# Two cross attentions whose row maxima are joined to the queries and whose scores are formed a second time, transposed

## The reference

```python
# layer 1                                            # layer 3: the same with biases on q, k, v, no mask, and
q = heads(x @ Wq); k = heads(ctx @ Wk); v = heads(ctx @ Wv)
scores = einsum('bhid,bhjd->bhij', q, k) * hd ** -0.5
scores = where(mask[:, None, None, :], scores, max_neg)
out = einsum('bhij,bhjd->bhid', softmax(scores), v).reshape(B, N, 256)
return out @ Wo                                      # relu(out @ W1 + b1) @ W2 + b2
```

## Time and profile before

| | us |
|---|---|
| runs | 1791.15, 1791.43, 1797.4 (median 1791.43) |
| profiled execution, span | 1785.6 |
| layer 1's cross attention, first scores to the last batch's `output_rows` | 659.05 to 831.19 |
| layer 3's, the same | 1351.67 to 1535.98 |
| busy over the span | PE 1579.5, DVE 941.3, ACT 717.5, POOL 409.0 |

### The profile page before, as it was taken

One profiled execution on the slowest core, in us unless ns is written; L12 is line 12 of the kernel. 1 busy time (PEld: TensorE's weight loads), 2 busy tenths in 40 slices (PEclk: granted clock), 3 DMA queues, 4 the chain that ended last, 5 costly groups with the idle time before them and its releaser, 6 DMA issues.

```text
span 1785.6 us, 40853 instructions
## 1 busy us (share of the span) xinstructions
PE 1579.5 (88%) x14786; PEld 1305.9 (73%) x14786; DVE 941.3 (53%) x2546; ACT 717.5 (40%) x1675; POOL 409.0 (23%) x627
## 2 busy tenths in 40 slices
PE   7998998799987879998797788997988999899998
PEld 6876776678975657776687566775876777689897
DVE  3665877511116657777110562556345667565864
ACT  3334876232323336652222314551755556211110
POOL 2224776500004421112000233432121111000101
PEclk9998999999998999998899798998998999999999
DMA  5343000278951011102686001001001000033232
GB/s 212 147 151 121 28 27 19 106 279 300 321 185 35 1 53 44 29 15 87 254 290 228 13 1 58 28 27 48 1 1 66 23 26 15 24 96 117 81 108 68
DMA packets 41852, 166.72 MB, mean 93 GB/s; under 512 B 5985, under 2 KB 16865, under 8 KB 30177
## 3 DMA queue, kind: packets, MB, share of 16 engines
q1 hardware_dynamic: 39392, 159.14, 25.7%
q0 software_dynamic: 2304, 5.51, 1.0%
HBM read 140.21 MB, written 24.41 MB: 92 GB/s over the span
## 4 chain that ended last, share of the span: by engine, by line
PE 70%; DVE 12%; issue 7%; DMA 3%; POOL 3%; ACT 3%; SPq 1%; DVEq 0%; POOLq 0%; ACTq 0%
PE bank L1688 7%; PE bank L1701 6%; PE bank L1268 6%; PE bank L1630 4%; PE bank L1255 4%; PE bank L1631 4%; PE bank L1632 4%; PE bank L1282 3%; PE bank L795 2%; PE bank L804 2%; PE bank L1238 2%; PE bank L1243 2%; PE bank L896 1%; PE bank L782 1%; DMA xrow<-slots 1%
## 5 line engine op out<-in xcount | busy, mean ns | idle before, releaser
L2053 ACT ACTIVATE arena<-big,nm 112x375 f32<-112x375 f32 x384 | 215.9, 605 | 29.5 <-DVE nm L2894 16.4
L1268 PEld LDWEIGHTS bank<-cst,arena 112*125 112x125 f32 x1152 | 146.6, 192 | 54.0 <-issue 29.0
L1268 PE MATMUL bank<-cst,arena 112*125 112x112 f32 x1152 | 168.0, 283 | 8.8 <-ACT big L2063 5.0
L3150 POOL TENSOR_TENSOR mv<-mv,cst 112x1 f32<-112x1 f32 x88 | 20.1, 228 | 607.3 <-DVE mv L2283 607.3
L2202 ACT ACTIVATE htile<-bank,wup 128x128 f32<-128x128 f32 x280 | 79.7, 368 | 189.7 <-PE bank L1688 189.6
L1688 PE MATMUL bank<-xtile,wup 128*128 128x128 f32 x1120 | 132.8, 278 | 0.3 <-DVE xtile L2997 0.2
L1688 PEld LDWEIGHTS bank<-xtile,wup 128*128 128x128 f32 x1120 | 129.8, 194 | 1.0 <-DVE xtile L2997 0.9
L3013 DVE COPY yrow<-bank 128x256 f32<-128x256 f32 x35 | 14.8, 424 | 217.5 <-PE bank L1701 217.5
L1701 PE MATMUL bank<-wdn,htile 128*128 128x256 f32 x560 | 126.3, 379 | 0.0
L2897 DVE TENSOR_SCALAR_CACHE_REDUCE big<-bank 112x375 f32<-112x375 f32 x192 | 96.0, 543 | 35.3 <-PE bank L1255 33.6
L1701 PEld LDWEIGHTS bank<-wdn,htile 128*128 128x128 f32 x560 | 103.9, 190 | 12.8
(11 more groups left out here) (359 smaller groups left out, 3571.7 us busy)
## 6 DMA issues: line engine op xcount, KB each, us to landing
wup<-in_moe_up SPq DMA_DIRECT2D x35, 1028.0 KB, 7.3
wdn<-in_moe_dn SPq DMA_DIRECT2D x35, 1024.0 KB, 6.1
vspace<-in_ring SPq DMA_DIRECT2D x40, 512.0 KB, 4.2
ctxs<-parts SPq DMA_DIRECT2D x30, 564.0 KB, 3.9
slots<-mlpw SPq DMA_DIRECT2D x11, 1024.0 KB, 6.5
parts<-ctxs SPq DMA_DIRECT2D x8, 564.0 KB, 3.1
xrow<-slots SPq DMA_DIRECT2D x35, 128.0 KB, 5.0
slots<-yrow SPq DMA_DIRECT2D x35, 128.0 KB, 7.0
```

Source lines behind the costliest of these rows:

```text
L1268: mm = pe.transpose(bank[4 + (3 * g + t) % 2][0:KT, j * T:(j + 1) * T], c_pr[:, g, j, t * KT:(t + 1) * KT], ident[0:T, 0:T])
L2053: nc.scalar.activation(c_pr[:, g, j, :], c_sc[:, g % 2, j, :], ACT.Exp, bias=nm[:, p, h:h + 1], scale=-1.0).then_inc(cexp_done, 1)
```

## The change

In layers 1 and 3 the program `cross_joined` takes the place of `cross` on every engine. VectorE only reads each bank of scores and stores the row minimum into `j_nm` (nothing is kept of the scores themselves). At the start of the next batch's steps TensorE transposes the minima of all 16 heads (`maxima`), and VectorE makes `j_q` from them and the negated queries (`maxima_in`): each head's 32 rows now hold 16 query rows and one row with the maxima. The keys are stored twice (`j_k`, one copy for even and one for odd heads), with ones in the row that meets the maxima, so that a second product (`scores_t`: for each of three thirds of the context 16 matmuls of 32 contraction rows, 125 x 112) gives scores minus maximum, already transposed. ScalarE takes the exponential from PSUM (12 of 125 x 448 per batch; in layer 1 the mask is a bias per context row, read from a new small input `mask_columns`). `transposes` and `tile` are gone. `values` runs once per batch, 48 matmuls, in the fourth step of the following batch. In that step the order on TensorE is: scores, queries of b + 1, values of b - 1, first half of the keys of b + 1, two thirds of the value rows of b, `rows_t` of b - 2. Banks: row scores in 3, 0, 1, 2, transposed scores in 3, 4, 5, 6 (6 is `OT`; 4 and 5 also take keys and value rows). Both parts now drain in 8 steps. `cross` is left for layer 0 alone, otherwise as it was. The core of the diff, with unchanged branches and small helpers cut:

```diff
+        self.ctx, self.joined = True, not clip and not qk_norm
...
+self.per.update({"c16": 16, "n1": 1, "m1": 1 if mlp else 0})
+        cols += [("keyhalf", 2), ("keyadd", 4)] if self.joined else [("bk", 2)]
...
+ROW_BANKS, TURNED_BANKS = (3, 0, 1, 2), (3, 4, 5, 6)
...
+    def scores(b, g, p):
+        if g == 0:
+            pe.wait_ge(cqm_ready, at(sub, "c1", b, 1))
+        if g % 2 == 0:
+            pe.wait_ge(ck_done, at(sub, "c2", b, g // 2 + 1))
+        pe.wait_ge(nexp_done, at(sub, "p12", b - 1, 4 * g - 3))
+        for j in range(4):
+            pe.wait_ge(cmax_ready, at(sub, "c16", b, 4 * g + j - 3))
+            if ROW_BANKS[j] == 0 and routed:
+                pe.wait_ge(route_in, 6 + routed)
+            rows = slice(32 * j, 32 * j + 32)
+            pe.matmul(bank[ROW_BANKS[j]][0:T, 0:S2], c_qm[rows, p, g // 2, g % 2, :], j_k[rows, p, g // 2, g % 2, :],
+                      start=True, stop=True).then_inc(cs_ready, 1)
+    def maxima(b, more):
+        pe.wait_ge(anm_clear, 3 + sub.index // 10)
+        pe.wait_ge(cmax_ready, at(sub, "c16", b, 16))
+        if more:
+            pe.wait_ge(cq_done, at(sub, "c1", b + 1, 1))
+        pe.wait_ge(xt_done, xt_at(sub, b - 2))
+        for g in range(4):
+            mm = pe.transpose(TL[:, g * T:(g + 1) * T], j_nm[:, g, :], ident[0:T, 0:T])
+        mm.then_inc(anm_ready, 1)
+    def scores_t(b, t, p, more):
+        pe.wait_ge(anm_done, at(sub, "n1", b, 1))
+        if more:
+            pe.wait_ge(cmax_ready, at(sub, "c16", b + 1, 4 * t + 1))
+        if t == 0:
+            pe.wait_ge(cv_done, at(sub, "c3", b, 3))
+            pe.wait_ge(cot_in, at(sub, "t1", b, 0))
+        for g in range(4):
+            for i in range(4):
+                if g == 0:
+                    pe.wait_ge(nexp_done, at(sub, "p12", b, 4 * t + i - 3))
+                rows = slice(32 * i, 32 * i + 32)
+                mm = pe.matmul(bank[TURNED_BANKS[i]][0:KT, g * T:(g + 1) * T],
+                               j_k[rows, p, g // 2, g % 2, t * KT:(t + 1) * KT], j_q[rows, g, :], start=True, stop=True)
+                if g == 3:
+                    mm.then_inc(ns_ready, 1)
+    def values(b, p):
+        pe.wait_ge(v_zero, 2)
+        pe.wait_ge(nexp_done, at(sub, "p12", b, 12))
+        for g in range(4):
+            for t in range(3):
+                for j in range(4):
+                    h = head_of(g, j)
+                    mm = pe.matmul(OT[32 * j:32 * j + 32, g * T:(g + 1) * T], vbuf[:, p, t, 32 * h:32 * h + 32],
+                                   j_p[:, t, j, g * T:(g + 1) * T], start=(t == 0), stop=(t == 2))
+        mm.then_inc(nv_done, 1)
...
+    def idle(b, n):
+        if isinstance(b, int) and b >= B:
+            pe.wait_ge(cmax_ready, at(sub, "c16", B - 1, 16))
+            for _ in range(n):
+                warm(bank[1], 256)
...
+    def step(b, g, p, back, more, one, two):
+        if g == 0:
+            if one:
+                maxima(b - 1, back[0])
+            if back[0]:
+                scores(b, g, p)
+                if one:
+                    pe.wait_ge(anm_done, at(sub, "n1", b - 1, 1))
+                value_rows(b, p, 0, TL)
+            if one:
+                idle(b, 2)
+                scores_t(b - 1, 0, 1 - p, back[0])
+            if two:
+                if back[0]:
+                    pe.wait_ge(cv_done, at(sub, "c3", b, 1))
+                elif one:
+                    pe.wait_ge(anm_done, at(sub, "n1", b - 1, 1))
+                else:
+                    pe.wait_ge(xt_done, xt_at(sub, b - 3))
+                output_rows(sub, b - 2)
+        if g == 1:
+            if back[0]:
+                scores(b, g, p)
+                if two:
+                    pe.wait_ge(con_step, at(sub, "t2", b - 1, 0))
+                else:
+                    pe.wait_ge(cv_done, at(sub, "c3", b, 1))
+                keys(b, p, 1, TL)
+            if one:
+                idle(b, 4)
+                scores_t(b - 1, 1, 1 - p, back[0])
+            if two:
+                if back[0]:
+                    pe.wait_ge(ck_done, at(sub, "c2", b, 2))
+                idle(b, 0 if one else 2)
+                output_columns(sub, b - 2)
+        if g == 2:
+            if back[0]:
+                scores(b, g, p)
+            if two:
+                if sub.mlp:
+                    hidden(b - 2)
+                else:
+                    project_rows(sub, b - 2)
+            if one:
+                idle(b, 2)
+                scores_t(b - 1, 2, 1 - p, back[0])
+            if two and sub.mlp:
+                project_hidden(b - 2)
+        if g == 3:
+            if back[0]:
+                scores(b, g, p)
+            if more:
+                if two:
+                    pe.wait_ge(ln_dve, u + 3 * (b - 2) + 1)
+                else:
+                    pe.wait_ge(ck_done, at(sub, "c2", b, 2))
+                q_in(b + 1, 1 - p, TL)
+            if one:
+                idle(b, 4)
+                values(b - 1, 1 - p)
+            if more:
+                keys(b + 1, 1 - p, 0, bank[4])
+            if back[0]:
+                pe.wait_ge(cq_done, at(sub, "c1", b, 1))
+                for t in (1, 2):
+                    value_rows(b, p, t, bank[5][:, (t - 1) * DM:t * DM])
+            if two:
+                if more:
+                    pe.wait_ge(cq_done, at(sub, "c1", b + 1, 1))
+                idle(b, 0 if one else 4)
+                rows_t(sub, b - 2, p)
+        if sub.index == 4 and isinstance(b, int) and b >= B - 2:
+            route(b, g)
+    cross_steps(pe, step, 8)
...
+    def keys(b, p, m, src):
+        act.wait_ge(ck_ready, at(sub, "c2", b, m + 1))
+        for e in range(2):
+            ins = nc.scalar.activation(j_k[:, p, m, e, :], src[:, 0:S2], ACT.Identity, scale=w(sub, "keyhalf")[:, e:e + 1],
+                                       bias=w(sub, "keyadd")[:, 2 * m + e:2 * m + e + 1])
+        ins.then_inc(ck_done, 1)
...
+    def exps(b, t, p):
+        if t == 0:
+            act.wait_ge(nv_done, at(sub, "v1", b, 0))
+            if sub.mask:
+                act.wait_ge(crow_ready, b + 1)
+        for i in range(4):
+            act.wait_ge(ns_ready, at(sub, "p12", b, 4 * t + i + 1))
+            src = bank[TURNED_BANKS[i]][0:KT, 0:4 * T]
+            if sub.mask:
+                ins = nc.scalar.activation(j_p[:, t, i, :], src, ACT.Exp, bias=mask_add[:, p, t:t + 1])
+            else:
+                ins = nc.scalar.activation(j_p[:, t, i, :], src, ACT.Exp)
+            ins.then_inc(nexp_done, 1)
...
     def step(b, g, p, back, more, one, two):
+        if g == 0 and back[0]:
+            value_rows(b, p, 0, 1, TL)
+        if g == 1 and back[0]:
+            keys(b, p, 1, TL)
+        if g == 2 and two and sub.mlp:
             hidden(b - 2)
+        if g < 3 and one:
+            exps(b - 1, g, 1 - p)
+        if g == 3:
+            if more:
+                q_in(b + 1, 1 - p, TL)
+                keys(b + 1, 1 - p, 0, bank[4])
+            if back[0]:
+                value_rows(b, p, 1, 2, bank[5])
+            if two:
+                rows_in(B + sub.base["row"], b - 2)
         if sub.index == 4 and isinstance(b, int) and (b, g) in ((B - 2, 3), (B, 0)):
             route_exps(1, 0 if b < B else 1)
+    cross_steps(act, step, 8)
...
+    def scores_in(b, g, p, js):
+        for j in js:
+            h = 4 * g + j
+            dve.wait_ge(cs_ready, at(sub, "c16", b, h + 1))
+            apart(dve)
+            at_max = j_nm[:, g, 32 * j + 16 - 16 * (g % 2):32 * j + 17 - 16 * (g % 2)]
+            src = bank[ROW_BANKS[j]][0:T, 0:S2]
+            if sub.mask:
+                if h == 0:
+                    dve.wait_ge(crow_ready, b + 1)
+                    apart(dve)
+                dve.wait_ge(cmax_ready, at(sub, "c16", b, h - 1))
+                apart(dve)
+                ins = dve.tensor_tensor_reduce(j_sum[:, j % 2, :], src, j_row[:, p, :], 1.0, -LOWEST,
+                                               ALU.add, ALU.min, at_max)
+            else:
+                ins = dve.tensor_reduce(at_max, src, AX_X, ALU.min)
+            ins.then_inc(cmax_ready, 1)
+    def maxima_in(b, p):
+        dve.wait_ge(anm_ready, at(sub, "n1", b, 1))
+        dve.scalar_tensor_tensor(out=j_q.rearrange("p g n -> p (g n)"), in0=c_qm[:, p, :, :, :].rearrange("p m e n -> p (m e n)"),
+                                 scalar=-1.0, in1=TL[:, 0:4 * T], op0=ALU.mult, op1=ALU.add).then_inc(anm_done, 1)
...
+    def step(b, g, p, back, more, one, two):
+        if g == 0:
+            if two:
+                output_in(sub, b - 2, nv_done, at(sub, "v1", b - 1, 0))
+            if one:
+                maxima_in(b - 1, 1 - p)
+            if sub.index == 4 and isinstance(b, int) and b == B:
+                route(sub, 7.5)
+            if back[0]:
+                scores_in(b, g, p, range(4))
+        if g == 1:
+            if back[0]:
+                scores_in(b, g, p, (0,))
+            if two:
```

(40 more changed lines are left out.)

395 lines of the change are left out of this document (211 added, 184 removed).

## The result

The changed kernel takes 1819.43 us (median of 4 runs, 1817.3 to 1819.71) against 1794.41 (4 runs, 1791.15 to 1798.04) on the same chip: ratio 1.0136, 95% interval 1.0116 to 1.0155. The forecast was 1790 with a range of 1772 to 1808; the time lies above the range. The profiled span grew from 1785.6 to

A forecast was written before the change was run, and what follows sets the result against it. The order and length of TensorE's pieces were taken to bound both stages. Layer 1's +3.2 and layer 3's -4.4 us sum to -1.2, from 1785.6 to 1784.4 profiled, forecast as a median of 1790, range 1772 to 1808.

The forecast's parts named there:

- Bound and throughput: Both stages: TensorE's pieces set the time; its work falls 2.95 us per batch, giving 35 us over 12 batches if gapless.
- A steady batch, the waits: Layer 1's steady batch: TensorE waits about 4.5 us in sum, including 1.5 at the keys and 1.25 at `maxima`.
- Rival (b): Steady batches: half of the waits at keys and `maxima` vanish, 17 us less, 1773 in all; chance 0.28.
- A steady batch, the prices: TensorE's time from piece to piece: four row scores 0.83 us, keys 0.8, transposed scores 1.05; VectorE reads after 1.07.
- the walk: One steady layer 1 batch followed piece by piece from `maxima`: period 20.5 us against 20.15 before.
- Rival (c): Handovers between engines around bank 3 cost more than taken; 0.5 us more each gives 1811; chance 0.19.
- the ring of bank 3: Three times per batch: TensorE's product goes to ScalarE, back to TensorE's scores, then to VectorE; last scores wait 0.8 us.
- Fill: Batches 0 and 1 of both stages: batch 0 takes 11.9 us, batch 1 17.4; -3.3 in layer 1, -3.4 in layer 3.
- Rival (d): Steady periods: TensorE's waits lower its granted clock to a mean of 0.96, +14 us, 1804 in all; chance 0.08.
- Batches 6 and 7, drain: Layer 1's end: batches 6 and 7 take 46.0 us with routing's 6 us as before, -0.3; the drain +3.4.
- Start: Before the first scores: one key product less, -1.0 us per stage.
- Tail, layer 3's end: Layer 1's routing tail +3 us, bounds 0 and 4; layer 3's batch 7 with drain 39.1 against 35.6, +3.5.

The follow-up runs named there:

- e5: Changed kernel with VectorE normalising the output of two batches ago before the first new row minimum; ratio 1.0054 to the kernel before, layer 1 period 20.87 us.
- e6: Changed kernel with `rows_t` and its copy ahead of the keys in the fourth step; ratio 1.0064 to the kernel before, layer 1 period 21.16 us.
- e3: Changed kernel with TensorE's instructions of both joined stages written out instead of looped; ratio 1.0122 to the kernel before, layer 1 period 21.30 us.
- e12: Changed kernel with early second keys and warm products in batch 0, normalisation before row minima, `rows_t` before keys, TensorE written out; ratio 0.9907 to the kernel before.
- e4: Changed kernel with layer 1's row minima taken by a plain reduction without the mask's row; ratio 1.0119 to the kernel before, layer 1 period 21.75 us.
- e8: Changed kernel with layer 1's routing operations one step later in batch 7 and behind batch 6's normalisation in the drain; ratio 1.0107 to the kernel before.

## Why the prediction was wrong

**Bound and throughput.** Right: in all steady batches TensorE's own order sets the time, VectorE and ScalarE are under 12 us of 22. The waits eat what the removed transposes give.

**A steady batch, the waits.** Right in place, close in size: e5 took 1.31 and e6 1.02 out of the period, where the forecast had 1.5 and 1.25. All waits of the period shown add up to 3.5 us (0.57, 1.23, 0.24, 0.70, 0.79), against the forecast's about 4.5, so they can't be what made the period longer. Rival (b) said that half of the two large waits would not be there; the changed kernel has them in full.

**A steady batch, the prices.** This is the step that failed most: "From one piece's start to the next on TensorE: four row scores 0.83". The prices came from rows in which TensorE had not waited. In the loop of the changed kernel three of the four row scores take 1.12 to the next piece, and the transposed scores of the first step 1.38. e3 and e12 show that this goes when the loop is written out, 1.2 us of TensorE's work per batch (18.51 to 17.28). A second part was in the walk from piece to piece itself. The throughput count leaves 20.05 - 2.95 = 17.1 us of work, and e3's 17.28 bears it out; the walk, 20.5 with 4.5 of waits, has only 16.0, and the two were not compared. One price in it was misread, the keys at 0.8; a timeline of before has 0.95 from the keys to the next piece:

```profile
718.77 1.11 PE L1238 MATMUL bank<-ctxs,kv 128*128 128x376 f32 x5
719.72 1.02 PE L1268 MATMUL bank<-cst,arena 112*125 112x112 f32 x8
```

In the changed kernel they take 1.06 and 0.97, twice per batch. VectorE's first read lies 1.45 behind the first scores, not 1.07; e4 takes 0.22 of these 0.38 away. Per period that is 1.7 over the 20.5, and in layer 3 0.9 over the 22.6: 8.1 instead of 1.4 in four batches, 0.3 instead of -3.5 in five. Rival (c) had the right form, a handover that costs more than I take, and at d = 0.5 gave 1811; but it blamed the product, which by itself takes 1.14 where I had 1.05, and the ring of bank 3, whose wait is 0.70 where I had 0.8. The sign for it, a period above 21.5, came without it. Its chance of 0.19 was too small for a price taken too low somewhere.

**Fill.** The 11.9 for batch 0 ("16 row minima at 0.47, with the second keys' copies between step 1 and 2") failed twice over: VectorE stood idle for 3.3 us behind the second keys and their copies, and with little work on TensorE the granted clock fell to 0.50. e12 gives 12.8 and 12.2 with both mended, so the count of row minima was nearly sound; the wait was priced too low, and the clock was put at nothing. Batches 0 and 1 took 6.6 us more than forecast in layer 1 and 5.3 in layer 3; of the 6.6, 0.9 lie in batch 1. Rival (d) had the clock, but looked for it in the steady batches, where it stayed at 1.00 in the changed kernel. The section A second HAM failure mode: psum-queue depth-cycling of TensorE: Matmul & The Clock Gate in the Trainium skill, cited for (d), would have the clock oscillate under frequent short gaps; in the loops with gaps of 0.2 to 1.2 us the traces mostly do not agree (1.00 in 91 of 96 steady batches), in batch 1 of layer 1 with gaps of 0.3 to 0.9 some do (below).

**Batches 6 and 7, drain.** The forecast kept "the routing's 6 us of now". But routing operations that were hidden before now stand ahead of VectorE's normalisation, which TensorE's keys need: 3.3 us idle and then half clock. In the drain they held the normalisation again, and the clock stood at 0.91; e8 has 16.4 there, where the forecast said 12.65 + 3.4 = 16.1. The prices of the loop have no part in batches 6 and 7, which are written out in both kernels; of their 50.8 us (46.0 forecast) batch 6 has 24.97 at a granted clock of 0.93 and batch 7 25.83 at 0.80. Moving the operations only moved batch 7's wait, and what else these two batches cost stays open.

**Start.** -1.0 per stage was wrong: one key product less on TensorE, but ScalarE has two key copies (1.22 us together) ahead of the queries', and the first scores wait for GpSimd behind these. This was read from the trace and not tested.

**Tail, layer 3's end.** +3 and +3.5 forecast, +2.2 and +2.5 measured: close. No run takes these terms apart.

## What to carry to other kernels

Take the price of a piece from a row where its engine has just waited, if it will wait in the new order: in a loop with computed semaphore counts the same four matmuls took 0.90 or 1.19. If a forecast counts TensorE's work in two ways, compare the two: 17.1 and 16.0 us of the same batch showed a fault before any run. When work is taken out of a pipeline's first step, look at what TensorE does meanwhile, for the time can go twice, once in the wait and once by the clock behind it. A change of order is worth judging again once its few named waits are mended: each edit was a few lines, the gains added up, and 1.4% slower became 0.9% faster.
